# Attention steps of the next block moved by one slot, behind the down products and in front of the next gate products

## The reference

```python
x = x + _layernorm(attention(_layernorm(x)))
#   attention: q, k, v = x Wq', x Wk', x Wv'  (8 heads of 32)
#   per chunk of 64 tokens: o = q state + tril(q k') v;  state += k' v
#   o / max(|sum(q * cumsum(k))|, 1), rmsnorm over a head, then Wo
x = x + _layernorm(ffn(_layernorm(x)))
#   ffn: gate = x Wg[e], up = x Wu[e], h = silu(gate) * up   (8 experts, 256 wide)
#   out = sum over e of weight[t, e] * (h Wd[e]);  weight from a sigmoid router
```

## Time and profile before

| | us |
|---|---|
| median of the runs | 1549.72 |
| the profiled execution | 1550.57 |
| its span, first to last instruction | 1548.9 |
| PE busy | 1514.9 (98%) |
| DVE busy | 1005.0 (65%) |
| ACT busy | 683.1 (44%) |
| POOL busy | 446.4 (29%) |

### The profile page before, as it was taken

One profiled execution on the slowest core, in us unless ns is written; L12 is line 12 of the kernel. 1 busy time (PEld: TensorE's weight loads), 2 busy tenths in 40 slices (PEclk: granted clock), 3 DMA queues, 4 the chain that ended last, 5 costly groups with the idle time before them and its releaser, 6 DMA issues. The chain is left out here.

```text
span 1548.9 us, 35779 instructions
## 1 busy us (share of the span) xinstructions
PE 1514.9 (98%) x13648; PEld 1308.9 (85%) x13648; DVE 1005.0 (65%) x2388; ACT 683.1 (44%) x1264; POOL 446.4 (29%) x720
## 2 busy tenths in 40 slices
PE   7799999999999999999999999999999999999997
PEld 6688888888888888888888888888888888888886
DVE  4656656666666666756666666666666666666665
ACT  4543444445344453534445344453535445344433
POOL 1422413224141232413224141232413224141231
PEclk9999999999999999999999999999999999999999
DMA  4300000000000000000000000000000000000000
GB/s 116 103 1 2 28 0 14 14 14 14 0 14 14 14 14 0 27 0 14 14 14 14 0 14 14 14 14 0 24 3 14 14 14 14 0 14 16 1 8 21
DMA packets 25343, 24.56 MB, mean 16 GB/s; under 512 B 2016, under 2 KB 25056, under 8 KB 25312
## 3 DMA queue, kind: packets, MB, share of 16 engines
q1 hardware_dynamic: 25312, 24.13, 4.8%
HBM read 15.74 MB, written 8.39 MB: 16 GB/s over the span
## 5 line engine op out<-in xcount | busy, mean ns | idle before, releaser
L927 DVE TENSOR_TENSOR late<-late,up_ps 128x512 f32<-128x512 f32 x256 | 175.1, 684 | 173.2 <-PE up_ps L418 142.4
L418 PE MATMUL down_ps<-w_hi,h_hi 128*128 128x256 f32 x976 | 266.7, 295 | 0.0
L1130 POOL TENSOR_TENSOR rms_f<-rms_in,minus_half 128x16 f32<-128x16 f32 x32 | 93.7, 2929 | 588.8 <-DVE rms_in L891 588.8
L726 ACT ACTIVATE late<-gate_ps 128x512 f32<-128x512 f32 x256 | 152.2, 595 | 241.5 <-PE gate_ps L418 235.5
L418 PE MATMUL down_ps<-w_hi,h_lo 128*128 128x256 f32 x976 | 253.4, 281 | 0.0
L644 ACT ACTIVATE h_hi<-late 128x512 fp32r<-128x512 f32 x256 | 160.7, 628 | 189.2 <-DVE late L927 189.2
L949 DVE SCALAR_TENSOR_TENSOR late<-down_ps,route,late 128x256 f32<-128x256 f32 x364 | 158.9, 478 | 105.0 <-PE down_ps L418 102.4
L843 DVE TENSOR_TENSOR h_lo<-late,h_hi 128x512 fp32r<-128x512 f32 x256 | 175.8, 687 | 75.5 <-ACT h_hi L644 75.5
L418 PE MATMUL gate_ps<-ft_hi,w_hi 128*128 128x512 f32 x512 | 203.8, 398 | 0.6 <-ACT ft_hi L644 0.4
L418 PE MATMUL up_ps<-ft_hi,w_hi 128*128 128x512 f32 x512 | 203.8, 398 | 0.0
L418 PE MATMUL up_ps<-ft_hi,w_lo 128*128 128x512 f32 x512 | 203.1, 397 | 0.0
(11 more groups left out here) (159 smaller groups left out, 2667.3 us busy)
## 6 DMA issues: line engine op xcount, KB each, us to landing
xs<-in_x SPq DMA_DIRECT2D x32, 256.0 KB, 2.8
out_rows<-late SPq DMA_DIRECT2D x32, 256.0 KB, 2.2
late<-in_wg SPq DMA_DIRECT2D x8, 256.0 KB, 2.9
late<-in_wu SPq DMA_DIRECT2D x8, 256.0 KB, 2.8
late<-in_wd SPq DMA_DIRECT2D x8, 256.0 KB, 2.8
late<-in_wkv_t SPq DMA_DIRECT2D x1, 512.0 KB, 5.5
late<-in_wq_t SPq DMA_DIRECT2D x1, 256.0 KB, 4.4
late<-in_wo_t SPq DMA_DIRECT2D x1, 256.0 KB, 5.0
```

The costliest lines, as they stand in the source:

```text
L418: last = nc.tensor.matmul(dst, lhs, rhs, start=n == 0, stop=n == len(terms + low_terms) - 1)
L726: nc.scalar.activation(h_f[:, m, :], gate_ps[:, :], ACT.Silu).then_inc(silu_ready[0], 1)
L927: nc.vector.tensor_tensor(h_f[:, m, :], h_f[:, m, :], up_ps[m][:, :], ALU.mult).then_inc(h_ready[0], 1)
L1130: nc.gpsimd.tensor_tensor(rms_f[:, p, :, :], rms_in[:, :, :], minus_half[:, :, :], ALU.pow)\
```

## The change

Only the list STEPS is changed; FIRST_STEPS and the code are not. An empty slot 0 is put in front, so that the steps with products, which stood in even slots (between up and down), stand in odd ones (between down and the next gate), and steps without products move from odd slots to even ones. Toward the end the list is brought back to 28 slots: the entry of keep_x1 goes to the head of slot 5, where it is with q1 and kv1; ft0 joins ln3_apply1 in slot 25; ln3_apply1, ft1 and ft_out keep their slots 25 and 26. In the slot with ln3_apply0 and ln2_apply1 (now 23) the two change places.

```diff
 STEPS = [
+    [],
     [("xt", 0), ("xt", 1)],
     [],
     [("kv", 0), ("q", 0)],
     [],
-    [("q", 1), ("kv", 1)],
-    [("keep_x1",)],
+    [("keep_x1",), ("q", 1), ("kv", 1)],
+    [],
     [("kt", 0), ("su", 0)],
     [],
     [("s", 0), ("kt", 1)],
...
     [("ln2_apply", 0)],
     [("wo", 1), ("ln2_add", 0), ("ln3_stats", 0)],
     [("ln2_stats", 1)],
-    [("ln3_apply", 0), ("ln2_apply", 1)],
+    [("ln2_apply", 1), ("ln3_apply", 0)],
     [("ln2_add", 1), ("ln3_stats", 1)],
-    [("ft", 0)],
-    [("ln3_apply", 1)],
+    [("ft", 0), ("ln3_apply", 1)],
     [("ft", 1), ("ft_out", 0), ("ft_out", 1)],
     [],
 ]
```

## The result

The changed kernel takes 1650.55 us (median; 1649.73 to 1651.43), the kernel before in the same comparison 1549.15 (1548.34 to 1550.41): ratio 1.0655, interval 1.0643 to 1.0666, or 101.4 us more. The prediction was 1631, range 1603 to 1652: slower, at the two places it named, and near the upper end of the range. The profiled execution took 1651.27 us, its span is 1649.5, its mean granted clock 0.981.

What follows compares the result with a forecast made beforehand. PE was taken to set the time, so new PE waits count: 22.5 (kv0) + 3.9 (ot1) + 45.3 (end of the pass) + 0.5 (start) + 9.3 (clock) = 81.5 us, giving 1631 us, range 1603 to 1652.

Steps and rivals of the forecast that it cites:

- a fall of the clock in all 15 passes: Rival: PE's clock falls in nearly every pass behind the wait for ft1; 1645 us, chance 0.12.
- 0.5 us a pass of thin cover: Slots 3 to 15: handovers cost 0, or up to 0.5 us a pass if their cover is thinner than read.
- What bounds the kernel: PE sets the time; its gate, up and down groups take 1.39, 1.40 and 1.43 us, with one 0.30 stall a pass.
- Entry costs: s and o behind a down group: entry costs 0 to 0.09 us, worth 0 to -0.36 a pass; taken as 0.
- rival "faster": ft1's 0.30 stall and 0.36 of entry costs go in each pass: 9.9 us less, 1540 us, chance 0.04.
- xt in slot 1: xt's DVE part stands behind route_rank, so kv0 waits 1.61 us in 14 of 15 passes: 22.5 us.
- Slots 3 to 15, keep_x1: Moved products and keep_x1 ahead of q1 and kv1 in slot 5: no handover later than its product, cost 0.
- norm_apply1: Slot 18: it stands behind hidden(5,1), so PE waits 0.26 us at ot1, 15 times: 3.9 us.
- The end of the pass: Chain from wo1 to ft1 loses one down group; stalls at ft0, gate(7,1) and ft1 add 3.02 us a pass, 45.3 us.
- the second chain: From ln2_add1's start to ln3_apply1's, through DVE and POOL, 3.99 us; ft1 follows 1.24 later, stall 2.83.
- The clock: Behind the wait for ft1 PE may drop to 1.2 GHz, losing 1.55 us; taken in 6 of 15 passes, 9.3 us.
- The rival without it, at 1622: No fall of PE's clock behind the new stalls: 1622 us, chance 0.17.

Runs made afterwards that it cites:

- after: The kernel with the whole change to STEPS, against the kernel before: 1650.55 us against 1549.15, ratio 1.0655.
- xt_alone: The kernel before with only the two xt steps moved from slot 0 to slot 1: 1606.97 us against 1550.49, ratio 1.0363.
- head_moved: The kernel before with the new order in slots 0 to 11 only, the old order behind: 1572.22 us, ratio 1.0142.
- fill12: The changed kernel with 12 filler products on PE in front of ft1's transposes: 1634.08 us, ratio 1.0539.
- stats_early: The changed kernel with ln2_stats1 moved from slot 22 to slot 21, behind ln3_stats0: 1626.09 us, ratio 1.049.
- end_moved: The kernel before with the new order in slots 12 to 27 only, the old order ahead: 1634.55 us, ratio 1.0542.
- swap_back: The changed kernel with slot 23 in the old order, ln3_apply0 ahead of ln2_apply1: 1642.47 us, ratio 1.06.

## Why the prediction was right, and what it mis-sized

**The number.** The direction and the places were right, the size was not: 81.5 us forecast, 101.4 measured. 1650.55 lies 1.5 below the upper end of the range, and that it lies inside is luck in part. The upper end was made of a fall of the clock in all 15 passes and 0.5 us a pass of thin cover; there were 9 falls and no such cost. What came in their place were two things that the prediction didn't have: POOL's root beside low_hidden, and falls that last twice as long.

**What bounds the kernel.** Right: PE's groups kept their 1.39, 1.40 and 1.43 us, and all that was lost are waits of PE and its clock.

**Entry costs.** Taken as 0. In after the down group in front of s takes 1.52 us from start to start, 0.09 more than 1.43, as the up group did. So nothing is won or lost, and the -0.36 of the rival "faster" is out.

**xt in slot 1.** Right: 1.52 for 1.61 (1.62 with the longer kv0 group), and only in the 14 passes with out_stats. xt_alone and head_moved show it by itself.

**Slots 3 to 15, keep_x1.** Right: no wait of PE between kv0 and ot1, and head_moved's pass is the old one plus kv0's wait. keep_x1 ended at 697.70 in the pass whose xt starts at 680.15, 17.6 us behind it (forecast: 661 - 643.38 = 17.6); q1's copy stood straight behind it (ACT, in order of time), and PE waited for neither.

```profile
696.64 1.06 ACT L644 ACTIVATE late<-x 128x1024 f32<-128x1024 f32 x1 [0.33 <-DMA out_rows<-late]
697.61 0.58 ACT L644 ACTIVATE q_t<-att_ps 128x512 f32<-128x512 f32 x1
```

**norm_apply1.** Right: 0.28 for 0.26.

**The end of the pass.** Right in place and order, 0.73 us a pass too small: 3.75 for 3.02. The step that failed is "from its start to ACT's ln2_apply1 it takes 2.91 through POOL", and the 3.99 of the second chain "with the same DVE work beside it". Both durations held only for the old alignment of DVE to POOL. ln2_stats1 went behind hidden(6,1), and so POOL's root onto DVE's low_hidden: the first chain took 0.58 more, which is ft0's 0.93 in place of 0.37. In the second chain the DVE work beside the root was not the same: hidden(7,0), 0.69 us, no longer stood between ln3_stats1 and add_down, and low_hidden met another instruction of the root, 0.22 more. From wo1 to ft1 that is 762.53 - 746.73 = 15.80 us where 15.01 were forecast, 0.58 + 0.22 with 0.01 lost in rounding. gate(7,1)'s forecast wait of 0.12 did not come: it starts at 756.50, 0.06 us behind the end of silu(7,0) at 755.87 + 0.57 = 756.44, where the prediction took 0.15.

**The clock.** Right that it falls in some passes, 8.9 us too small: 9 falls for 6, and four of them last 6.83 us and cost 2.61 where rows 10 had shown only 3.41 and 1.55. fill12 shows the term by itself. The rival without it, at 1622, is out. The Trainium skill (TensorE: Matmul & The Clock Gate, section "Why this matters for your kernels") warns only of idle gaps longer than those in the rows here. The runs differ: waits of 2.36 us (2.19 idle by the row) brought the clock down in 11 of 15 passes of stats_early, and the 2.23 of rows 10 once. Waits of 0.3 and 1.5 us never did.

**What stays open.** Why the same wait in front of ft1 brings the clock down in 9 passes of after, in 14 of end_moved, and in every pass of swap_back. In end_moved and swap_back the falls come 99.0 us apart, nearly the length of a pass. In after the four long falls begin 1.92 to 1.95 us behind PE's last product before the wait (761.50 against 762.53 - 2.96 = 759.57), so with ft1 still 1.0 us away, and the five short ones 2.56 to 2.98 us behind it. So the place of a wait in time may matter as well as its length, but no run moved the waits without changing something else. Of the small change, 0.06 us a pass has no cause shown either.

## What to carry to other kernels

In a hand-written order, moving a product to where its own engine is free moves its copies on the other engines too, and each lands behind whatever stands in that slot there: one xt step put behind 5 us of DVE work cost some 56 us, about 12 of them through the clock, with PE's own work unchanged. Walk the chain of handovers with the durations of the trace, but don't carry a duration over from one alignment to another where two engines that hinder each other (here POOL and DVE) are moved against each other. And a wait of PE can have a second price in its clock: waits of 2.2 us and more by PE's idle time had it here in many passes, 1.3 to 2.6 us each, and waits of 1.5 in none. Where it can't be removed, fill it with no more products than it is long, for each one beyond that is paid in full.

## What the runs showed of the hardware that I had not expected

- POOL beside DVE. A POOL instruction on 128 x 2 elements takes 0.71 us, and 1.29 when DVE's 0.68 us low_hidden, whose two operands lie in SBUF, starts within 0.05 us of it; one of 0.20 takes 0.55 when low_hidden starts 0.16 earlier, and ends 0.05 behind it. The Trainium skill (SBUF — State Buffer, section "Who interferes with whom") says that a DVE instruction with two SBUF inputs contends with a GpSimd instruction that reads SBUF, and that the order of issue decides which of the two is held up. The row at 754.70 agrees, and so does the one at 718.19, which ends 0.06 behind DVE's low_hidden; in the rows at 752.19 POOL starts 0.04 ahead by the record and is the longer one all the same, so which of them holds the other can't be told from its start alone.
- The clock. In after the lower level lasted 3.41 or 6.83 us and cost 1.55 or 2.61. The same wait of 3.12 us brought it about more often in a shorter pass (15 falls in swap_back, 9 in after), so taking 1.0 us out of a pass gave 8 us in place of 15 until fillers held the clock.
- A filler product of float32 128 x 128 takes 0.21 us, start to start.
